# Gathers that wait for their own row tile, and context rows added by two engines in the last two batches, in a one-core transformer kernel

## Chip, cores and metric

One Trainium2 chip, one core. The metric is device time in microseconds (us) of one launch. The kernel is written instruction by instruction for five engines (TensorE, VectorE, ScalarE, GpSimd and SyncE, which issues loads); the engines meet only at semaphores. In the profile they are PE (PEld for its weight loads), DVE, ACT, POOL and SP.

## What is computed

The input `x` has 8 batches of 512 rows of 256 numbers (f32), the context 64 rows for each batch. Four steps follow each other, each of the form `x = x + tanh(g) * f(layernorm(x))`:

```python
x = x + tanh(g0) * cross_attention(ln(x), ctx)           # biased by fside
x = x + tanh(g1) * experts(ln(x))                        # a shared expert, and the best 2 of 8 by a router
# the step that this change is about, for each batch:
txt_proj = ctx @ Ws                                      # 64 x 256
feat_proj = ln(x) @ W                                    # 512 x 256
h = tanh(txt_proj[:, None] + feat_proj[None] + b)        # 64 x 512 x 256
rho = h . w                                              # 64 x 512, then masked and a softmax over the 64
txt_h = softmax(rho) @ ctx
x = x + tanh(g2) * (tanh(txt_h @ Wcw + bcw) * ln(x) + tanh(txt_h @ Wcb + bcb))
x = x + tanh(g3) * (quantized(ln(x)) @ ternary + bias)
```

## The kernel before

**Work.** All rows of `x` stay in SBUF. The kernel runs through three stages that overlap. In the first, batch by batch, attention, routing and the shared expert are done, and each row is scattered to DRAM at two places, sorted by expert. In the second, 71 "routed tiles" of 128 rows follow: each loads its rows and 1.5 MB of its expert's weights, goes through `turn_rows`, `gate`, `up`, `gate_act` and `narrow`, and its result is stored to DRAM by a DMA that POOL issues (`narrow` on POOL, L554). In the third, for each batch b the results come back: eight gathers (two for each of the four row tiles of 128 rows; L566, POOL), eight `add` steps (DVE, L953), a layer norm (`stats`, `aggr`, `power`, `newton`, `scale`, `turn`; DVE, but the power is POOL's, L534, and the transposes are PE's), and `feature` (PE L1278, copied by DVE at L960 to `featT`).

**Units.** The `tanh` of a batch is cut into 64 units (two halves ec of the 256 columns, 32 numbers m). A unit is 128x1024: two context rows against 512 rows of x. ACT does it as two instructions of 128x512 (L643, L644), each with the context row as its bias. PE then multiplies the unit by `w` (`sum`, L1291, eight matmuls). A ring of 16 buffers holds units (`wide`): unit u may be written when the sum of unit u-16 is done. After the last unit of a batch comes `mix_out` (softmax over rho, the affine, a layer norm, quantizing, the ternary product, the output).

**Units added beforehand.** For the last two batches (b of 6 and 7) `added(b, m)` is true for odd m. There DVE adds the context rows first (`preadd`, L969 and L970, two 128x512 tensor_scalar instructions, from and to SBUF, with a per-partition scalar), and ACT needs one instruction of 128x1024 (L635) in place of two.

**Order.** `Plan` writes down every step of the work at a place on one line, and each engine executes its steps in the order of these places, after `LAGS` has shifted a kind of step on one engine. Engines do not reorder: a step that waits holds all that is behind it on that engine. Places are counted in slots. The third stage begins at slot 0 of this text (`zero` in the code): batch b has slots 64b to 64b+64, and one unit has one slot. A routed tile has 8 slots, tile 22 begins at slot 0. On POOL and PE, `narrow` of tile r stands at 8r - 161.3: that of tiles 68, 69 and 70 (the last) at 382.7, 390.7 and 398.7. `tanh` of unit i of a batch is at 64b + i + 0.5 with a lag of 1.5 on ACT, `preadd` of unit i at 64b + i - 2, less 1.5 on DVE.

**The way into a batch before.** `mix_in` places the eight gathers, the adds, the norm and `feature` as equal steps: for batch 0 from slot -46 to -1, for a later one from 39.5 slots before its first slot to 3 before it. The add of gather j stands five steps behind it. The first gather of a batch waits until every tile that any row of the batch can lie in is stored: for batch 0 the first 15 tiles:

```python
tiles = 2 * ST * (b + 1) + E - 1
if j == 0:
    e.wait_ge(s_found, b + 1)
    for r in range(OUTS):
        e.wait_ge(s_stored[r], 16 * len(range(r, tiles, OUTS)))
```

Of the kernel before, what the change touches and what calls it, by code (L numbers as in the profile page):

```python
# [9 lines left out]
ALU = mybir.AluOpType  # L10
# [23 lines left out]
PLACES = {"attend": 72, "route": 36, "late": -59, "mix_first": -46, "mix_in": 24.5, "mix_in_end": -3, "feature": 3, "sum": 5,  # L34
          "mix_out": 8.5, "mix_out_end": 52.5}
# [5 lines left out]
    "scalar": {"gate_act": -2.5, "soft_rho": 1, "softmax": -2, "spread": 7.5, "squash": 2, "tanh": 1.5, ("turn", "mix"): -0.5,  # L41
               "turn_e": 1.5},
    "vector": {"add": 0.5, "add_bias": 1.5, "affine": 0.5, ("aggr", "att"): 2.5, ("aggr", "lin"): -0.5, "choice": -1.5,
               "convert": -10.5, "find": 3, "gate_act": 3, "linear": 1.5, "narrow": 2, ("newton", "att"): 2, ("newton", "lin"): 2,
               ("newton", "mix"): 0.5, ("newton", "moe"): 1, "place": -0.5, ("power", "att"): 3, "preadd": -1.5, "quantize": 1,
               ("scale", "moe"): -0.5, "side": 3.5, "softmax": 0.5, ("stats", "att"): 2.5, "step": 2, "sums": 2.5, "text": 10.5,
               ("turn", "moe"): -0.5, "turn_q": 1.5, "turn_rows": 2, "weigh": -1, "weigh_ws": -0.5},
    "tensor": {"count": -1.5, "scores": -0.5, "spread": 2.5, "sum": 1, "text": 1.5, ("turn", "mix"): -0.5, "weigh": -2},
# [3 lines left out]
class Plan:  # L52
# [16 lines left out]
    def chain(self, name, b, steps, start, end):  # L69

        self.chains[name, b] = {s for step in steps for s in step}
        self.place(steps, start, end)
# [70 lines left out]
    def added(self, b, m):  # L143

        return b >= self.B - 2 and m % 2 == 1

    def arrange(self):
# [7 lines left out]
        for b in range(B):  # L155
            at = PERIOD * b
            self.chain("attend", b, self.attend(b), at - PLACES["attend"], at - PLACES["attend"] + PERIOD - 2)
            self.chain("route", b, self.route(b), at - PLACES["route"], at - PLACES["route"] + PERIOD)
# [15 lines left out]
        for b in range(B):  # L174
            at = zero + N * b
            if b == 0:
                place([[("find", b)]], at - 60, at - 60)
                self.chain("mix_in", b, self.mix_in(b), at + PLACES["mix_first"], at - 1)
            else:
                place([[("find", b)]], at - N + 18, at - N + 18)  # L180
                self.chain("mix_in", b, self.mix_in(b), at - N + PLACES["mix_in"], at + PLACES["mix_in_end"])
# [8 lines left out]
            if b < B - 1:  # L190
                self.chain("mix_out", b, self.mix_out(b), at + N + PLACES["mix_out"], at + N + PLACES["mix_out_end"])
            else:
                self.chain("mix_out", b, self.mix_out(b), at + N + 1, at + 2 * N)
# [54 lines left out]
def build(nc, a):  # L248
# [20 lines left out]
    with ctx:  # L269
# [123 lines left out]
        s_wide_in, s_wide, s_sum = sem("wide_added"), sem("wide_tanh"), sem("rho_product")  # L393
# [113 lines left out]
        def gpsimd(e):  # L507
# [20 lines left out]
            for name, *k in plan.of["gpsimd"]:  # L528
# [13 lines left out]
                elif name == "pad":  # L542
# [3 lines left out]
                    for j in range(h * E // 2, (h + 1) * E // 2):  # L546
                        e.indirect_dma_start(
                            out=rows_dram, out_offset=bass.IndirectOffsetOnAxis(ap=pad_at[:, j:j + 1], axis=0),
                            in_=zero_tile[:, :], in_offset=None).then_inc(s_padded, 16)
                elif name == "narrow" and is_routed(k[0]):  # L550
# [4 lines left out]
                elif name == "gather":  # L555
# [3 lines left out]
                    tiles = 2 * ST * (b + 1) + E - 1  # L559
# [806 lines left out]
```

## Time and profile before

| what | us |
|---|---|
| three runs | 1123.75, 1125.29 (median), 1131.14 |
| the profiled execution, its own time | 1128.25 |
| its span, first to last instruction | 1126.5 |
| ACT busy in the span | 704.4 |
| PE / DVE / POOL busy | 1007.1 / 664.9 / 213.4 |
| mean granted TensorE clock, of full speed | 0.970 |

The busy times are sums over the whole span. The three stages have different limits, so they have to be read from windows of the trace, not from this table.

### The profile page before, as it was taken

Reading aid. Unit: us, or ns where it says so; the run is one execution under the profiler, and the core shown is the slowest. Engines: PE = TensorE matmul, PEld = TensorE weight load, DVE = VectorE, ACT = ScalarE, POOL = GpSimd, SP = SyncE. Lnnn points to the kernel's source line nnn. Section 1 sums busy time; section 2 is a strip of 40 time slices with the busy share of each in tenths; the row PEclk is TensorE's granted clock in tenths of the full one; section 3 lists DMA queues with packets and bytes.
Section 4 is the critical chain, followed back from the end, with each engine's and each line's share of the span. In section 5 each row is a group of like instructions: output and inputs, shape, how many; then the busy total and the mean of one; then the engine's idle time right before and its main releaser. Section 6 shows DMA issues by size and latency. Waiting matters only on the chain.

```text
span 1126.5 us, 23210 instructions
## 1 busy us (share of the span) xinstructions
PE 1007.1 (89%) x8772; PEld 768.6 (68%) x8772; DVE 664.9 (59%) x1902; ACT 704.4 (63%) x1154; POOL 213.4 (19%) x257
## 2 busy tenths in 40 slices
PE   6789999999889999999999999999999999948561
PEld 2467777778779998877777777777777777513120
DVE  2567778887723345434276266366366466796746
ACT  1211111111101110699999999999999999999990
POOL 1033212333320003031030030030030030120000
PEclk9969999999989999999999999999999999989995
DMA  8011110111167999766466466466466564010000
GB/s 247 24 61 61 52 40 32 43 38 38 43 239 243 336 335 340 265 228 200 139 231 215 144 223 216 156 211 215 166 202 214 176 197 145 21 33 20 1 20 19
DMA packets 114050, 164.19 MB, mean 146 GB/s; under 512 B 13235, under 2 KB 70068, under 8 KB 113940
## 3 DMA queue, kind: packets, MB, share of 16 engines
q1 hardware_dynamic: 104004, 135.57, 36.3%
q0 software_dynamic: 9936, 27.15, 6.6%
q8 instruction: 70, 1.15, 0.4%
q14 instruction: 40, 0.33, 0.1%
HBM read 138.69 MB, written 23.99 MB: 144 GB/s over the span
## 4 chain that ended last, share of the span: by engine, by line
PE 53%; ACT 27%; DVE 11%; issue 8%; DMA 0%; POOL 0%; SPq 0%; POOLq 0%; DVEq 0%
PE bank L1108 16%; PE bank L1291 9%; PE bank L1270 8%; PE bank L1113 5%; ACT tanhs L644 4%; ACT tanhs L643 4%; ACT arena L643 3%; ACT arena L644 3%; PE bank L1261 3%; ACT shared_w L644 2%; ACT shared_w L643 2%; PE bank L1150 2%; PE bank L1094 2%; PE bank L1165 2%; ACT tanhs L635 2%
## 5 line engine op out<-in xcount | busy, mean ns | idle before, releaser
L1108 PE MATMUL bank<-rowsT,expert_w 128*128 128x128 f32 x2272 | 277.1, 275 | 0.5 <-DVE rowsT L917 0.5
L1108 PEld LDWEIGHTS bank<-rowsT,expert_w 128*128 128x128 f32 x2272 | 270.0, 192 | 7.2 <-issue 3.3
L628 ACT ACTIVATE act<-bank 128x512 f32<-128x512 f32 x103 | 63.5, 616 | 217.3 <-PE bank L1108 112.6
L934 DVE COPY rows_out<-bank 128x256 f32<-128x256 f32 x71 | 30.1, 424 | 192.8 <-PE bank L1270 192.8
L1270 PE MATMUL bank<-expert_w,act 128*128 128x256 f32 x568 | 139.4, 388 | 0.8 <-issue 0.8
L554 POOL DMA_DIRECT2D expert_rows<-rows_out x71 | 40.2, 566 | 511.6 <-DVE rows_out L934 511.0
L643 ACT ACTIVATE tanhs<-arena,txtT 128x512 f32<-128x512 f32 x168 | 128.3, 764 | 4.3 <-DVE arena L960 4.3
L644 ACT ACTIVATE tanhs<-arena,txtT 128x512 f32<-128x512 f32 x168 | 128.3, 764 | 0.0
L1113 PE MATMUL bank<-normT,shared_w 128*128 128x256 f32 x512 | 125.0, 392 | 0.0
L1270 PEld LDWEIGHTS bank<-expert_w,act 128*128 128x128 f32 x568 | 102.3, 190 | 32.7 <-issue 21.7
L643 ACT ACTIVATE arena<-arena,txtT 128x512 f32<-128x512 f32 x144 | 110.0, 764 | 0.0
L644 ACT ACTIVATE arena<-arena,txtT 128x512 f32<-128x512 f32 x144 | 109.9, 764 | 0.0
L1113 PEld LDWEIGHTS bank<-normT,shared_w 128*128 128x128 f32 x512 | 97.1, 196 | 16.9 <-issue 3.3
L1291 PE MATMUL bank<-tanhs,pick_w 128*32 128x256 f32 x1536 | 97.1, 382 | 12.8 <-ACT tanhs L644 7.0
L1291 PE MATMUL bank<-arena,pick_w 128*32 128x256 f32 x1280 | 88.8, 391 | 13.3 <-ACT arena L644 6.8
L539 POOL DMA_INDIRECT rows_by_expert<-arena,slot_of x64 | 63.5, 992 | 133.7 <-DVE slot_of L844 116.6
L1291 PEld LDWEIGHTS bank<-tanhs,pick_w 128*32 128x32 f32 x1536 | 45.3, 109 | 59.4 <-ACT tanhs L644 13.1
L924 DVE SCALAR_TENSOR_TENSOR act<-act,bank 128x512 f32<-128x512 f32 x103 | 70.9, 688 | 11.6 <-DVE act L922 0.5
L1291 PEld LDWEIGHTS bank<-arena,pick_w 128*32 128x32 f32 x1280 | 38.6, 111 | 48.3 <-ACT arena L644 12.1
L922 DVE SCALAR_TENSOR_TENSOR act<-act,bank 128x512 f32<-128x512 f32 x103 | 69.7, 677 | 0.9 <-ACT act L628 0.9
L566 POOL DMA_INDIRECT picked<-expert_rows,found_at x64 | 64.3, 1005 | 28.6 <-issue 18.4
L1261 PE MATMUL bank<-shared_w,act 128*128 128x256 f32 x256 | 63.6, 392 | 6.8 <-DVE act L924 6.8
(232 smaller groups left out, 1444.0 us busy)
## 6 DMA issues: line engine op xcount, KB each, us to landing
expert_w<-in_WgT SPq DMA_DIRECT2D x71, 512.0 KB, 4.0
expert_w<-in_WuT SPq DMA_DIRECT2D x71, 512.0 KB, 5.2
expert_w<-in_WdT SPq DMA_DIRECT2D x71, 512.0 KB, 6.7
rows_in<-rows_by_expert SPq DMA_DIRECT2D x71, 128.0 KB, 5.4
expert_rows<-rows_out POOLq DMA_DIRECT2D x71, 128.0 KB, 4.3
x<-in_x SPq DMA_DIRECT2D x8, 512.0 KB, 5.5
out<-x SPq DMA_DIRECT2D x16, 256.0 KB, 4.7
score<-in_fside SPq DMA_DIRECT2D x8, 128.0 KB, 2.3
```

The costliest lines, as they stand in the source:

```text
L539: e.indirect_dma_start(out=rows_dram, out_offset=bass.IndirectOffsetOnAxis(ap=slot_of[j][:, ST * b + i:ST * b + i + 1], axis=0), in_=held[ ...
L566: e.indirect_dma_start(out=picked[u % PICKED][:, :], out_offset=None, in_=outs_dram[0:tiles * P, :], in_offset=bass.IndirectOffsetOnAxis(a ...
L628: e.activation(act[n % 2][:, :], banks[2 * (n % 2)][:, :], ACT.Tanh, scale=0.5).then_inc(s_tanh, 1)
L643: e.activation(w[:, 0:S], featT[ec], ACT.Tanh, bias=txtT[:, ec, t:t + 1])
L644: e.activation(w[:, S:2 * S], featT[ec], ACT.Tanh, bias=txtT[:, ec, t + 1:t + 2]).then_inc(s_wide, 1)
L922: link(e.scalar_tensor_tensor(out=h[:, :], in0=h[:, :], scalar=1.0, in1=bg[:, :], op0=ALU.add, op1=ALU.mult))
L924: linked(lambda: e.scalar_tensor_tensor(out=h[:, :], in0=h[:, :], scalar=0.5, in1=bu[:, :], op0=ALU.mult, op1=ALU.mult)).then_inc(s_h, 1)
L1108: got = e.matmul(bank[:, i * P:(i + 1) * P], w[:, at:at + P], t[:, c * P:(c + 1) * P], start=c == 0, stop=c == DC - 1)
L1113: got = e.matmul(bank[:, i * HALF:(i + 1) * HALF], shared_w[:, at:at + P], normT[b % 2][:, c * S + h * HALF:c * S + (h + 1) * HALF], start ...
L1261: got = e.matmul(shared_bank[:, i * D:(i + 1) * D], act[n % 2][:, c * HALF + i * P:c * HALF + (i + 1) * P], shared_w[:, at:at + D], start= ...
L1270: got = e.matmul(row_bank[:, 0:D], act[n % 2][:, c * P:(c + 1) * P], w[:, at:at + D], start=c == 0, stop=c == IC - 1)
L1291: got = e.matmul(rho_bank[32 * j:32 * j + 32, 0:H], pick_w[:, ec, 31 - m:63 - m], wide[u % WIDE][:, j * H:(j + 1) * H], start=(ec, m) == ( ...
```

## The change

The first gather of each row tile of 128 rows waits, and only for the tiles that rows up to its own row tile can lie in: for batch 0 these are 9, 11, 13 and 15 tiles for row tiles 0 to 3. Gathers, adds and the statistics (now one row tile at a time) become a chain of their own (`collect`): each add stands two steps behind its gather. For batch 0 it runs from slot -71 to -25.5, and the rest of the norm and `feature` from -25.5 to -1. For a later batch, collecting runs from 53 to 20 slots before its first slot, the rest from 20 to 3 before it. The second `feature` (ec of 1) moves from slot 3 to slot 20 of the batch, and `feature` gets a lag of -2 on PE. `find` of batch 0 moves from slot -60 to -70, with its lag of 3 on DVE.

In the last two batches every unit is added beforehand: odd m by DVE, at i - 1.5 less 1.5, and even m by POOL, at i - 3. Each engine has a semaphore of its own for this. A number of other lags change.

```diff
-PLACES = {"attend": 72, "route": 36, "late": -59, "mix_first": -46, "mix_in": 24.5, "mix_in_end": -3, "feature": 3, "sum": 5,
-          "mix_out": 8.5, "mix_out_end": 52.5}
+PLACES = {"attend": 72, "route": 36, "late": -59, "gather_first": -71, "norm_first": -25.5, "gather": 11, "norm": 44, "mix_in_end": -3,
+          "feature": 20, "sum": 5, "vector": 1.5, "gpsimd": 3, "mix_out": 8, "mix_out_end": 50.5}
...
# LAGS, the entries that change:
# scalar: squash 2 -> 0.5
# vector: convert -10.5 -> -20.5, linear 1.5 -> 5, (newton, mix) 0.5 -> 1, side 3.5 -> -3.5, (stats, mix) 0 -> 1.5,
#         step 2 -> 0.5, sums 2.5 -> 3.5
# tensor: feature 0 -> -2, text 1.5 -> 7
...
+    def collect(self, b):
+
+        steps = []
+        for i in range(self.ST + 1):
+            for j in range(2):
+                steps.append(([("gather", b, 2 * i + j)] if i < self.ST else []) + ([("add", b, 2 * i - 2 + j)] if i else []))
+            if i:
+                steps[-1].append(("stats", "mix", b, i - 1))
+        return steps
+
     def mix_in(self, b):
-        pairs = 2 * self.ST
-        steps = [[("gather", b, j)] + ([("add", b, j - 5)] if j >= 5 else []) for j in range(pairs)]
-        return steps + [[("add", b, j)] for j in range(pairs - 5, pairs)] + self.norm("mix", b) + [[("feature", b, 0)]]
+        return self.norm("mix", b)[1:] + [[("feature", b, 0)]]
...
     def added(self, b, m):
 
-        return b >= self.B - 2 and m % 2 == 1
+        if b >= self.B - 2:
+            return ("gpsimd", "vector")[m % 2]
+        return None
...
             for i, (ec, m) in enumerate(pairs):
                 if self.added(b, m):
-                    place([[("preadd", b, ec, m)]], max(at, at + i - 2), max(at, at + i - 2))
+                    early = max(at, at + i - PLACES[self.added(b, m)])
+                    place([[("preadd", b, ec, m)]], early, early)
...
+                elif name == "preadd" and plan.added(k[0], k[2]) == "gpsimd":
+                    preadd(e, "gpsimd", *k)
...
                 elif name == "gather":
-                    tiles = 2 * ST * (b + 1) + E - 1
+                    tiles = 2 * (ST * b + j // 2 + 1) + E - 1
                     if j == 0:
                         e.wait_ge(s_found, b + 1)
+                    if j % 2 == 0:
                         for r in range(OUTS):
                             e.wait_ge(s_stored[r], 16 * len(range(r, tiles, OUTS)))
...
                     if plan.added(b, m):
-                        e.wait_ge(s_wide_in, wide_in_no[u] + 1)
+                        e.wait_ge(s_wide_in[plan.added(b, m)], wide_in_no[u] + 1)
                         e.activation(w, w, ACT.Tanh).then_inc(s_wide, 1)
...
+        def preadd(e, engine, b, ec, m):
+
+            u = unit_of(b, ec, m)
+            w = wide[u % WIDE]
+            bank, use, _ = misc["feature", b, ec]
+            e.wait_ge(s_misc[bank], use)
+            if u >= WIDE:
+                e.wait_ge(s_sum, u - WIDE + 1)
+            t = b * T + 2 * m
+            e.tensor_scalar(w[:, 0:S], featT[ec], txtT[:, ec, t:t + 1], None, ALU.add)
+            e.tensor_scalar(w[:, S:2 * S], featT[ec], txtT[:, ec, t + 1:t + 2], None, ALU.add).then_inc(s_wide_in[engine], 1)
...
                     elif kind == "mix":
-                        e.wait_ge(s_added, 2 * ST * (b + 1))
+                        e.wait_ge(s_added, 2 * ST * b + 2 * part[0] + 2)
...
-                    for i in range(ST):
+                    for i in part or range(ST):
                         link(e.bn_stats(own["stats"][:, i, :], xt(b)[:, i, :]))
```

## Rows read from the trace of the kernel before

**Rows 1.** Busy us by stretch: PE, PEld, DVE, ACT, POOL; then clock, DMA share, GB/s

```profile
500.00:600.00 100.00, 98.52 (x1063) 74.71 (x1062) 50.73 (x132) 100.00 (x169) 19.34 (x23) 1.00 0.60 201
958.15:1028.00 69.85, 49.71 (x597) 25.12 (x595) 59.70 (x161) 69.85 (x100) 13.10 (x13) 0.93 0.10 30
1028.00:1099.40 71.40, 46.58 (x595) 15.98 (x591) 41.66 (x114) 71.34 (x101) 1.53 (x1) 0.98 0.03 9
```

**Rows 2.** Waits from 461 to 955 us: total us, times, longest

```profile
ACT tanhs L643 <- DVE arena L960: 4.3, 1, 4.3
```

**Rows 3.** Timeline of ACT where the first batch's units begin

```profile
start us, us, engine line op out<-in xcount [idle before <-releaser]
461.38 0.72 ACT L643 ACTIVATE tanhs<-arena,txtT 128x512 f32<-128x512 f32 x1 [4.29 <-DVE arena L960]
...
465.07 0.58 ACT L628 ACTIVATE act<-bank 128x512 f32<-128x512 f32 x1
```

**Rows 4.** Timeline of ACT: first unit of batch 6, and three of batch 7

```profile
958.15 0.85 ACT L643 ACTIVATE tanhs<-arena,txtT 128x512 f32<-128x512 f32 x1
...
1070.07 1.04 ACT L635 ACTIVATE tanhs<-tanhs 128x1024 f32<-128x1024 f32 x1
1071.02 0.71 ACT L643 ACTIVATE arena<-arena,txtT 128x512 f32<-128x512 f32 x1
...
1072.24 1.04 ACT L635 ACTIVATE arena<-arena 128x1024 f32<-128x1024 f32 x1
```

**Rows 5.** Timeline of DVE around the adds of batch 0

```profile
423.53 0.42 DVE L934 COPY rows_out<-bank 128x256 f32<-128x256 f32 x1 [3.09 <-PE bank L1270]
...
429.05 0.42 DVE L934 COPY rows_out<-bank 128x256 f32<-128x256 f32 x1 [3.09 <-PE bank L1270]
...
435.74 0.48 DVE L953 SCALAR_TENSOR_TENSOR x<-picked,share,x 128x256 f32<-128x256 f32 x1 [4.26 <-DMA picked<-expert_rows,found_at]
...
437.63 0.42 DVE L934 COPY rows_out<-bank 128x256 f32<-128x256 f32 x1
```

**Rows 6.** Timeline of PE: after these adds, and around the first feature product

```profile
438.19 0.41 PE L1223 MATMUL bank<-ident,rows_in 128*128 128x128 f32 x2 [1.87 <-issue]
...
456.95 1.95 PE L1108 MATMUL bank<-rowsT,expert_w 128*128 128x128 f32 x16
458.73 1.88 PE L1278 MATMUL bank<-mixT,feat_w 128*128 128x512 f32 x4
```

**Rows 7.** Timeline of POOL: first two gathers, and the last three stores

```profile
429.76 1.02 POOL L566 DMA_INDIRECT picked<-expert_rows,found_at  x1 [4.97 <-DMA expert_rows<-rows_out]
431.09 0.97 POOL L566 DMA_INDIRECT picked<-expert_rows,found_at  x1 [0.30 <-issue]
...
959.47 0.61 POOL L554 DMA_DIRECT2D expert_rows<-rows_out  x1 [9.87 <-DVE rows_out L934]
970.75 0.54 POOL L554 DMA_DIRECT2D expert_rows<-rows_out  x1 [10.67 <-DVE rows_out L934]
977.15 0.74 POOL L554 DMA_DIRECT2D expert_rows<-rows_out  x1 [5.86 <-DVE rows_out L934]
```

**Rows 8.** POOL's groups by form: its only elementwise work without the power

```profile
L514 POOL TENSOR_SCALAR_AFFINE_SELECT ident<-ident 128x128 f32<-128x128 f32 x1 | 0.3, 284 | 0.2 <-POOL ident L511 0.2
L511 POOL MEMSET ident<- 128x128 f32 x1 | 0.2, 205 | 0.3 <-POOLq L1356 0.3
L1356 POOL MEMSET const-float32-1.0<- 128x1 f32 x1 | 0.1, 97 | 0.0
```

**Rows 9.** Timeline: a power of POOL beside DVE's added units, and one alone

```profile
1062.37 0.48 DVE L969 TENSOR_SCALAR tanhs<-arena,txtT 128x512 f32<-128x512 f32 x1
1062.77 0.48 DVE L970 TENSOR_SCALAR tanhs<-arena,txtT 128x512 f32<-128x512 f32 x1
...
1062.55 1.53 POOL L534 TENSOR_TENSOR ln_lin_r<-ln_lin_var,halves 128x4 f32<-128x4 f32 x1 [47.28 <-DVE ln_lin_var L737]
...
1111.07 1.01 POOL L534 TENSOR_TENSOR ln_lin_r<-ln_lin_var,halves 128x4 f32<-128x4 f32 x1 [46.99 <-DVE ln_lin_var L737]
```

More of the change, by code:

```diff
@@ L40 @@
     "gpsimd": {},
-    "scalar": {"gate_act": -2.5, "soft_rho": 1, "softmax": -2, "spread": 7.5, "squash": 2, "tanh": 1.5, ("turn", "mix"): -0.5,
+    "scalar": {"gate_act": -2.5, "soft_rho": 1, "softmax": -2, "spread": 7.5, "squash": 0.5, "tanh": 1.5, ("turn", "mix"): -0.5,
                "turn_e": 1.5},
     "vector": {"add": 0.5, "add_bias": 1.5, "affine": 0.5, ("aggr", "att"): 2.5, ("aggr", "lin"): -0.5, "choice": -1.5,
[L44 to L48, printed above, removed]
+               "convert": -20.5, "find": 3, "gate_act": 3, "linear": 5, "narrow": 2, ("newton", "att"): 2, ("newton", "lin"): 2,
+               ("newton", "mix"): 1, ("newton", "moe"): 1, "place": -0.5, ("power", "att"): 3, "preadd": -1.5, "quantize": 1,
+               ("scale", "moe"): -0.5, "side": -3.5, "softmax": 0.5, ("stats", "att"): 2.5, ("stats", "mix"): 1.5, "step": 0.5,
+               "sums": 3.5, "text": 10.5, ("turn", "moe"): -0.5, "turn_q": 1.5, "turn_rows": 2, "weigh": -1, "weigh_ws": -0.5},
+    "tensor": {"count": -1.5, "feature": -2, "scores": -0.5, "spread": 2.5, "sum": 1, "text": 7, ("turn", "mix"): -0.5, "weigh": -2},
 }
@@ L67, in __init__, with chain @@
         self.count()
-    def chain(self, name, b, steps, start, end):
-        self.chains[name, b] = {s for step in steps for s in step}
-        self.place(steps, start, end)
+    def chain(self, name, b, *parts):
+        self.chains[name, b] = {s for steps, _, _ in parts for step in steps for s in step}
+        for part in parts:
+            self.place(*part)
     def check(self):
@@ L392, in build @@
         s_added = sem("x_expert_added")
-        s_wide_in, s_wide, s_sum = sem("wide_added"), sem("wide_tanh"), sem("rho_product")
+        s_wide_in, s_wide, s_sum = {e: sem(f"wide_added_{e}") for e in ("vector", "gpsimd")}, sem("wide_tanh"), sem("rho_product")
         s_rho, s_rho_sub, s_rho_e = sem("rho_read"), sem("rho_less_max"), sem("rho_exp")
@@ L716, in vector @@
                 elif name == "stats":
-                    kind, b = k
+                    kind, b, *part = k
                     own = ln_of(kind, b)
@@ L960, in vector @@
                     e.tensor_copy(featT[ec], bank[:, :]).then_inc(done, 1)
-                elif name == "preadd":
-                    b, ec, m = k
-                    u = unit_of(b, ec, m)
-                    w = wide[u % WIDE]
-                    bank, use, _ = misc["feature", b, ec]
-                    e.wait_ge(s_misc[bank], use)
-                    e.wait_ge(s_sum, u - WIDE + 1)
-                    t = b * T + 2 * m
-                    e.tensor_scalar(w[:, 0:S], featT[ec], txtT[:, ec, t:t + 1], None, ALU.add)
-                    e.tensor_scalar(w[:, S:2 * S], featT[ec], txtT[:, ec, t + 1:t + 2], None, ALU.add).then_inc(s_wide_in, 1)
+                elif name == "preadd" and plan.added(k[0], k[2]) == "vector":
+                    preadd(e, "vector", *k)
                 elif name == "rho":
```

21 lines of the change are left out of this document (12 added, 9 removed).

## The prediction

> **What bounds the kernel now.** I read the stretches first, then the waits, then the timelines. The table by stretch shows ACT busy for 100 of 100 us in the middle of the third stage, for 69.85 of 69.85 us in batch 6 and for 71.34 of 71.40 us in batch 7 [rows 1]. PE is nearly as full in the middle (98.52 of 100) but not in batches 6 and 7 (49.71 of 69.85, 46.58 of 71.40), since the last routed tile is stored at 977.15 [rows 7]. Between 461 and 955 us ACT's one wait for its tanh input is that ahead of the very first unit, 4.3 us [rows 2]. So from 461.38 us [rows 3] to about 1099.4, where the stretch of batch 7 ends, the time is ACT's work laid end to end, and PE has little to spare beneath it. What follows is the last output, some 27 us to the end of the span, which the change doesn't shorten. Two things can move the end: when the first unit starts, and what ACT spends on a unit.
>
> **What a unit costs ACT.** By start times, a unit of two instructions takes 1.22 us (1071.02 to 1072.24) and an added one 0.95 us (1070.07 to 1071.02) [rows 4]. A pair takes 2.17 us now and would take 1.90 with both added. 32 units in each of two batches change: 64 x 0.27 = 17.3 us less, 8.6 a batch. ACT does nothing else in that time, so all of it counts if the added units arrive in time. That is the question.
>
> **The start.** Today the first gather waits 4.97 us for the fifteenth tile's store [rows 7]. The first add then stands waiting on DVE (4.26 us), and the copy L934 of a routed tile stands behind it: it starts 8.58 us after the one before, where the regular distance is 5.52 [rows 5]. PE shows the same loss, with a 1.87 us idle ahead of its next transposes [rows 6]. That is 3.1 us. With a wait for 9 to 13 tiles and the first gather some 24 slots earlier, the stores are long done. A slot here is 5.52 / 8 = 0.69 us. A gather takes 6.0 us to land (429.76 to 435.74) [rows 5, 7]. The add stands two steps of 4.55 slots, 6.3 us, behind its gather in the plan, but the first gather is held by `find`, which comes to stand at slot -67, so DVE will still wait a little at the first two adds. DVE has 3.09 us free before each such copy [rows 5], which hides most of it. I count 2.5 of the 3.1 us as saved (0 to 3.1).
>
> Next, the first feature product stands behind the up product of tile 21 today (456.95, then 458.73) [rows 6]. With its new place (-4.75, where that up product has -4) it comes ahead of it, 1.8 us earlier. But three units later ACT does tile 22's gate activation (465.07 [rows 3]), whose product PE does not get to sooner by this, so I count 1.0. Start: **-3.5 us** (-5 to +1, since the moved lags of the first stage could also cost PE a little). The extra load on the DMA queues is nothing new: the same eight gathers run, only earlier. The adds and statistics are the same instructions, cut differently. In the middle batches gathers and the norm also move, but ACT has no gap there to close, so I put this at zero (-1 to +3: PE at 98.5% could be pushed behind ACT).
>
> **What POOL needs for a unit.** The trace has no tensor_scalar of POOL. The nearest rows are a memset of 128x128 (205 ns) against one of 128x1 (97 ns), 0.85 ns an element, and an affine_select, which also reads, with 284 ns, or 1.47 ns an element over the same start cost [rows 8]. For 512 elements that makes 0.53 and 0.85 us, so a unit of two costs 1.06 to 1.70 us. I take 0.65 an instruction, 1.3 a unit, nearer to the memset, since part of the affine_select's excess over it will be a fixed cost of reading. The Trainium skill's "GPSIMD Engine Reference" (section 3.1) gives 1.03 cycles an element for simple bodies bound by the port. With the memset's start cost that is an estimate of 0.54 us, and about 2 us less in the sum. POOL's rows for 128x128 neither reach this size nor have a scalar operand, so the trace can't say more.
>
> **Where POOL comes too late in batch 6.** POOL's queue is in order. (a) The store of tile 69 stands at slot 390.7, the added units from the tenth on behind it (10 - 3 = 7, slot 391). That store goes out at 970.75 and takes 0.54 [rows 7]. So unit 10 is ready at 971.3 + 1.3 = 972.6. At the new pace ACT would want it at 958.15 + 10 x 0.95 + 0.5 (one gate activation) = 968.1 [rows 4]: 4.5 us lost. It includes the first unit's own lateness, as that stands behind the store of tile 68 at 959.47. The store of tile 70 (977.15) is in time for the units behind it. (b) From slot 395 to about 420 batch 7's eight gathers come in between, 1.33 us apart (429.76 to 431.09) [rows 7]. In 24 slots POOL has 12 x 1.3 + 8 x 1.33 + 1.2 for a power = 27.4 us to do, ACT 12 x 1.90 = 22.8. Of the 4.6 missing, 1.1 are won back beforehand (three pairs at 1.90 - 1.3, less the 0.7 of a store): 3.5 lost. Batch 6: -8.6 + 4.5 + 3.5 = **-0.6 us** (with 1.06 a unit -3.7, with 1.70 +4.6). Batch 7 has only two powers beside its units: POOL 32 x 1.3 + 3 = 45 us, ACT 32 x 1.90 = 61. I leave 0.5 for late units: **-8.1 us**.
>
> **Sum.** -3.5 - 0.6 - 8.1 = -12.2 us from the profiled execution's own 1128.25 (span 1126.5 and 1.75 around it), 1116.05. That execution lies 2.96 us above the median of the runs shown, 1125.29, so the median should come to 1125.29 - 12.2 = **1113 us**. This kernel's times can be told from no change at about 1%, 11 us: the forecast is just beyond it.
>
> **Rival 1: POOL and DVE stand in each other's way, and it gets slower.** A power on four numbers takes 1.01 us alone and 1.53 us while DVE runs its adds end to end, 0.40 us apart [rows 9]. So there is something they share, and 0.52 us can be lost on one tiny instruction. The forecast has only some of this in its 1.3. If the two engines' large instructions exclude each other entirely, a pair costs 2 x 0.40 + 2 x 0.65 = 2.10 us, near the 2.17 of today. Other DVE work from SBUF comes on top: DVE is busy 59.70 us in batch 6 and 41.66 in batch 7 [rows 1], of which the 32 units are 32 x 0.80 = 25.6. If half of the rest excludes POOL too, that is 17 and 8 us. Batch 6: 67.2 + 17 + 10.6 (gathers) = 95 against 69.9, +25. Batch 7: 67.2 + 8 = 75 against 71.4, +4. With the start's -3.5: +25, **1151 us**. It decides from the point where a pair passes 2.17. Without the other DVE work: batch 6 +8, batch 7 -4, no change, **1125**. For it: rows 9. Against it: DVE's own instructions in the same row keep 0.48 us, so POOL waits there and not DVE, and exclusion need not last as long as an instruction's whole span. The Trainium skill's "SBUF — State Buffer" (section "Who interferes with whom") calls the port pair of these engines an exclusive lock, and whoever comes second blocks fully. By that rule, this rival is the outcome. The lengthened power agrees with a lock; how long one lasts, no row shows.
>
> **Rival 2: POOL is only slow.** At 1.70 a unit, batch 6 is +4.6 and batch 7 still holds 1.90 a pair but is late at its beginning, -7: with the start -6, **1119 us**. For it: the affine_select [rows 8].
>
> **Rival 3: POOL keeps up everywhere.** If its instructions overlap so that a unit takes 1.0 us or less and PE's stores come a little sooner, only some 3 us are lost in batch 6: -3.5 - 17.3 + 3 = -18, **1107 us**; with a start of -5 and no loss, 1103. Against it: the store of tile 69 is PE's to give.
>
> **How the numbers follow.** Forecast 0.45, spread 1108 to 1118; rival 1 0.22, of which 0.15 slower than 1136 and the rest near 1125; rival 2 0.18; rival 3 0.15. Faster by over 1% (below 1114): rival 3 and some six tenths of the forecast and a little of rival 2, 0.45. Slower by over 1%: 0.16. Within: 0.39. The range for 8 in 10 is 1103 to 1136, the upper end reaching into rival 1, the lower holding all of rival 3.
>
> **What would show it.** ACT's first unit near 457 us; L934 at its regular 5.5 us through the adds of batch 0. New L969 and L970 instructions on POOL, 0.55 to 0.75 us apart: above 0.95 apart, ACT is bound by POOL in both batches. Waits of ACT's L635 on POOL's units, 8 us in all, in batch 6, one right behind the last stores and one among batch 7's gathers, and almost none in batch 7. If instead L969 and L970 on DVE grow well beyond 0.48 us, rival 1 is at work. The forecast is wrong if ACT waits in batch 7, or if it starts its first unit no sooner.

## Result: 7.5% slower, because POOL sets the pace of both last batches

The changed kernel takes 1212.88 us (median of 4 runs, 1207.96 to 1213.43) against 1127.94 us for the kernel before in the same set of runs: ratio 1.0746, 95% interval 1.0694 to 1.0798. The forecast was 1113, its range ended at 1136, and the sign was wrong as well. The profiled execution takes 1213.38 us, its span is 1211.6, and the mean granted TensorE clock is 0.900 where it was 0.970.

In code lines of the changed kernel: `preadd` is L684 and L685 on both engines, the ACT instruction of an added unit L652, the pair of a unit not added L660 and L661, the store L570, the gather L583, the add L983, the copy of a routed tile L964, the copy to `featT` L990.

First the table of busy us by stretch, of the changed kernel, with columns as in [rows 1]:

```profile
500.00:600.00 100.00, 98.58 (x1086) 76.46 (x1079) 51.87 (x139) 100.00 (x168) 16.90 (x21) 1.00 0.58 197
955.00:1060.00 105.00, 46.74 (x450) 17.77 (x438) 73.23 (x138) 56.06 (x60) 103.24 (x67) 0.64 0.05 16
1060.00:1140.00 80.00, 45.97 (x398) 13.34 (x398) 48.42 (x94) 47.90 (x51) 80.00 (x49) 0.61 0.01 4
```

The middle of the third stage is what it was in [rows 1]: ACT 100 of 100 us, PE 98.58. From batch 6 on ACT, which was idle there for less than 0.1 us, works 56 of 105 and 48 of 80 us, and POOL, which had 13 and 1.5 us of work in a batch, is busy for 80 of 80. PE's granted clock has a mean of 0.64 and 0.61 in these stretches, so for most of the time it is at the lower of its two levels (1.2 and 2.4 GHz), while PE is busy for less than six tenths of the time. That is no cause of the loss: PE is waiting, as the next view shows.

The waits of the same kernel from 945 to 1190 us (total us, times, longest), those of ACT for its tanh input and one of PE's own:

```profile
PEld bank L1313 <- ACT tanhs L652: 39.6, 26, 3.5
ACT tanhs L652 <- POOL tanhs L685: 39.4, 23, 4.3
ACT arena L652 <- POOL arena L685: 35.4, 24, 2.5
...
ACT normT L652 <- POOL normT L685: 12.2, 8, 2.6
ACT shared_w L652 <- POOL shared_w L685: 11.7, 8, 2.3
```

ACT waits for POOL 63 times in 64 units, 98.7 us in all, and the sums on PE (L1313) wait for ACT. No row has ACT wait for an add of DVE. PE's longest waits are others, 41.5 us in two, for the output chain on DVE. They hold nothing up here: POOL, whose buffers PE's sums free, has 0.2 us of waits for PE in this window. The reason is in POOL's groups by form (busy us, mean ns of one):

```profile
L684 POOL TENSOR_SCALAR tanhs<-arena,txtT 128x512 f32<-128x512 f32 x24 | 41.8, 1743 | 0.3
L684 POOL TENSOR_SCALAR arena<-arena,txtT 128x512 f32<-128x512 f32 x24 | 40.9, 1706 | 0.1
```

One add costs POOL 1.71 us (219 us for all 128), not 0.65, and the instructions follow each other without a gap. The timelines of POOL and of ACT near 1088 us show the steady state:

```profile
1087.38 1.56 POOL L684 TENSOR_SCALAR arena<-arena,txtT 128x512 f32<-128x512 f32 x1
1088.91 1.56 POOL L685 TENSOR_SCALAR arena<-arena,txtT 128x512 f32<-128x512 f32 x1
```

```profile
1087.43 2.00 ACT L652 ACTIVATE arena<-arena 128x1024 f32<-128x1024 f32 x2 [1.33 <-POOL arena L685]
1090.51 2.00 ACT L652 ACTIVATE arena<-arena 128x1024 f32<-128x1024 f32 x2 [1.07 <-POOL arena L685]
```

ACT does two units in 2.00 us, then waits 1.07 until POOL has the next one: a pair takes 3.08 us at best, where the kernel before took 2.17 [rows 4].

The account of the two profiled executions closes with three numbers. ACT begins batch 6 at 954.84 (958.15 before): -3.3. From there to the end of its last unit it needs 228.9 us (to 1183.76) where it needed 141.2 (to 1099.34): +87.7. The rest of the span is 27.8 against 27.2: +0.7. Sum +85.1, the difference of the spans.

### The profile page after: what moved, and what is told of

Same layout as the page of the kernel before. It is cut to its first block, busy times and chain, and to the rows that moved or that the text cites. A ratio compares the mean times of both kernels' runs of the same rounds, so it can differ in the third digit from the quotient of the medians.

```text
span 1211.6 us, 23370 instructions
## 1 busy us (share of the span) xinstructions
PE 1031.8 (85%) x8772; PEld 770.8 (64%) x8772; DVE 716.5 (59%) x1902; ACT 693.2 (57%) x1090; POOL 427.8 (35%) x385
## 4 chain that ended last, share of the span: by engine, by line
ACT 34%; PE 33%; DVE 12%; issue 10%; POOL 9%; DMA 1%; SPq 0%; POOLq 0%; DVEq 0%
PE bank L1130 7%; ACT tanhs L661 6%; PE bank L1135 5%; ACT arena L660 5%; ACT tanhs L660 5%; ACT arena L661 5%; PE bank L1292 4%; PE bank L1313 3%; ACT shared_w L661 3%; PE bank L1283 3%; ACT shared_w L660 2%; ACT normT L660 2%; ACT normT L661 2%; PE bank L1116 2%; POOL tanhs L685 2%
## 5 line engine op out<-in xcount | busy, mean ns | idle before, releaser
L1130 PE MATMUL bank<-rowsT,expert_w 128*128 128x128 f32 x2272 | 276.7, 275 | 0.5 <-DVE rowsT L947 0.5
L1130 PEld LDWEIGHTS bank<-rowsT,expert_w 128*128 128x128 f32 x2272 | 270.4, 192 | 10.0 <-issue 6.2
L570 POOL DMA_DIRECT2D expert_rows<-rows_out x71 | 40.5, 570 | 497.0 <-DVE rows_out L964 497.0
L964 DVE COPY rows_out<-bank 128x256 f32<-128x256 f32 x71 | 30.0, 422 | 168.3 <-PE bank L1292 168.3
L1313 PE MATMUL bank<-tanhs,pick_w 128*32 128x256 f32 x1536 | 106.4, 423 | 20.6 <-ACT tanhs L652 20.6
L660 ACT ACTIVATE tanhs<-arena,txtT 128x512 f32<-128x512 f32 x144 | 111.1, 771 | 2.5 <-DVE arena L990 2.5
L661 ACT ACTIVATE tanhs<-arena,txtT 128x512 f32<-128x512 f32 x144 | 111.1, 771 | 0.0
L1313 PE MATMUL bank<-arena,pick_w 128*32 128x256 f32 x1280 | 93.4, 410 | 20.3 <-ACT arena L652 15.9
L660 ACT ACTIVATE arena<-arena,txtT 128x512 f32<-128x512 f32 x120 | 92.6, 772 | 0.0
L661 ACT ACTIVATE arena<-arena,txtT 128x512 f32<-128x512 f32 x120 | 92.6, 772 | 0.0
L1313 PEld LDWEIGHTS bank<-tanhs,pick_w 128*32 128x32 f32 x1536 | 46.8, 117 | 70.8 <-ACT tanhs L652 39.6
L1313 PEld LDWEIGHTS bank<-arena,pick_w 128*32 128x32 f32 x1280 | 35.5, 113 | 65.3 <-ACT arena L652 32.5
L583 POOL DMA_INDIRECT picked<-expert_rows,found_at x64 | 64.0, 1000 | 25.3 <-issue 17.3
L652 ACT ACTIVATE tanhs<-tanhs 128x1024 f32<-128x1024 f32 x48 | 48.5, 1053 | 39.4 <-POOL tanhs L685 39.4
```

Source lines behind the costliest of these rows:

```text
L583: e.indirect_dma_start(out=picked[u % PICKED][:, :], out_offset=None, in_=outs_dram[0:tiles * P, :], in_offset=bass.IndirectOffsetOnAxis(a ...
L652: e.activation(w, w, ACT.Tanh).then_inc(s_wide, 1)
L660: e.activation(w[:, 0:S], featT[ec], ACT.Tanh, bias=txtT[:, ec, t:t + 1])
L661: e.activation(w[:, S:2 * S], featT[ec], ACT.Tanh, bias=txtT[:, ec, t + 1:t + 2]).then_inc(s_wide, 1)
L1130: got = e.matmul(bank[:, i * P:(i + 1) * P], w[:, at:at + P], t[:, c * P:(c + 1) * P], start=c == 0, stop=c == DC - 1)
L1313: got = e.matmul(rho_bank[32 * j:32 * j + 32, 0:H], pick_w[:, ec, 31 - m:63 - m], wide[u % WIDE][:, j * H:(j + 1) * H], start=(ec, m) == ( ...
```

## Experiments

The ratios are to the kernel before in the same set of runs, whose median was 1128.05 us in the first set (e1 to e4), 1136.72 in the second (e5, e6, e7, e9), 1127.71 in the third (e8, e10) and 1135.33 in the fourth (e11, e5b).

### e1: all of the change but POOL's units

```diff
     def added(self, b, m):
-        if b >= self.B - 2:
-            return ("gpsimd", "vector")[m % 2]
+        if b >= self.B - 2 and m % 2:
+            return "vector"
```

> All of the change but POOL's added units: in the last two batches only odd m is added beforehand, by DVE, as before; gathers, places and lags are the new ones. If the whole loss comes from POOL's units and the first unit's earlier start (457.15 against 461.38 us) is kept to the end: 4 us faster than before, about 1124 us, and 85 to 90 us faster than the changed kernel. If the new places cost something in the middle batches or for the late units: no faster than before, 1128 us or more.

Measured: 1123.38 us, ratio 0.9959 [0.9938, 0.9981], which is -4.6 us, between -7.0 and -2.1. Batch 6 in its table by stretch:

```profile
952.27:1024.00 71.73, 50.76 (x586) 21.65 (x578) 58.37 (x159) 71.73 (x103) 12.48 (x12) 0.88 0.09 27
```

ACT is full in batch 6 again. So the new gathers, places and lags are worth a small gain, and the whole loss comes with POOL's units.

### e2: the kernel before, with POOL's units alone

The kernel before, with even m of the last two batches added by POOL as in the change (`"vector": 2, "gpsimd": 3` as places, two semaphores), and nothing else.

> The kernel before with POOL adding the even units of the last two batches, nothing else. If POOL's units are the whole loss: 1128 + 89 = about 1217 us. If they only hurt in the company of the new places and lags: well below 1200 us.

Measured: 1215.45 us, ratio 1.0776 [1.0742, 1.0811]. With e1 this makes the two parts of the change add up: 1.0776 x 0.9959 = 1.0732, and the whole change has 1.0746.

### e3: POOL's units, but none on DVE

```diff
-        if b >= self.B - 2:
-            return ("gpsimd", "vector")[m % 2]
+        if b >= self.B - 2 and m % 2 == 0:
+            return "gpsimd"
```

> The changed kernel with POOL's units but none of DVE's: odd m is left to ACT with its bias. Theory: POOL's instruction is slow by itself, 1.54 us start to start; its spans fall from a mean of 1.70 to nearly 1.56 us and 128 of them take 199 us in place of 218: about 1193 us, still POOL-bound. Rival: the two engines exclude each other and this sets POOL's pace; then without DVE's adds POOL's instructions fall well below 1 us, ACT is the bound again and the time is about 1125 us (1128 - 4, no saving on the odd units but the same on the even).

Measured: 1197.12 us, ratio 1.0609 [1.0583, 1.0635]. Taking all of DVE's adds away returns (1.0746 - 1.0609) x 1128 = 15.5 us. One stretch of it, and the durations of L684 on POOL (min/median/max ns, first and last start):

```profile
1060.00:1100.00 40.00, 27.84 (x250) 7.20 (x242) 8.48 (x19) 30.32 (x43) 40.00 (x27) 0.67 0.00 1
```

```profile
L684 POOL TENSOR_SCALAR tanhs<-arena,txtT x24: 1552/1553/1784, 947.0 to 1144.3; 128x512 f32<-128x512 f32 x24
```

With DVE busy for 8.48 of 40 us, POOL still works for 40.00 of 40, at 1.55 us an instruction. So POOL's own price is the cause, and what DVE does to it is the smaller part.

### e4: what POOL's instructions cost by themselves

The kernel before, with 19 POOL instructions ahead of everything, in which DVE does nothing (they are extra work, so its time of 1146.2 us has no meaning of its own). The comments stand here only; L530 to L534 are the other five kinds in their order.

```diff
+            kinds = [lambda to: e.tensor_scalar(to, fro, one, None, ALU.add)] * 3       # L528, scalar per partition
+            kinds += [lambda to: e.tensor_scalar(to, fro, 1.0, None, ALU.add)] * 3      # L529, constant
+            kinds += [lambda to: e.tensor_scalar(to[:, 0:256], fro[:, 0:256], one, None, ALU.add)] * 2
+            kinds += [lambda to: e.tensor_scalar(to[:, 0:128], fro[:, 0:128], one, None, ALU.add)] * 2
+            kinds += [lambda to: e.tensor_copy(to, fro)] * 3
+            kinds += [lambda to: e.memset(to, 0.0)] * 3
+            kinds += [lambda to: e.tensor_tensor(to, fro, other, ALU.add)] * 3
```

> The kernel before with 19 instructions of POOL ahead of everything, where DVE waits for POOL's constants and does nothing: 128x512 tensor_scalar with a per-partition scalar (3) and with a constant (3), the former with 256 and 128 columns (2 each), copy (3), memset (3) and tensor_tensor (3) of 128x512. Theory: the per-partition tensor_scalar takes 1.55 us alone too, some 3 ns an element (128 columns near 0.5 us), and the memset 0.53 us, as worked out from 128x128. Rival: alone it takes 0.6 to 0.8 us, and what the changed kernel shows is contention. The constant's form tells whether the scalar operand is what costs: then it takes about 0.6 us, else also 1.5. The whole kernel some 20 us longer than before.

POOL's groups by form from 4 to 23 us (busy us, mean ns):

```profile
L528 POOL TENSOR_SCALAR arena<-tanhs 128x512 f32<-128x512 f32 x3 | 4.7, 1566 | 0.1
L529 POOL TENSOR_SCALAR arena<-tanhs 128x512 f32<-128x512 f32 x3 | 4.4, 1488 | 0.0
L534 POOL TENSOR_TENSOR tanhs<-tanhs 128x512 f32<-128x512 f32 x3 | 3.7, 1264 | 0.0
L530 POOL TENSOR_SCALAR arena<-tanhs 128x256 f32<-128x256 f32 x2 | 1.8, 928 | 0.0
L533 POOL MEMSET tanhs<- 128x512 f32 x3 | 1.5, 532 | 0.0
...
L531 POOL TENSOR_SCALAR arena<-tanhs 128x128 f32<-128x128 f32 x2 | 1.2, 608 | 0.0
L532 POOL COPY arena<-tanhs 128x512 f32<-128x512 f32 x2 | 1.2, 616 | 0.0
```

The memset of 512 comes out at 532 ns, just where the prediction's 0.85 ns an element had put it, and a copy at 616. The tensor_scalar takes 608, 928 and 1566 ns for 128, 256 and 512 elements: (1566 - 608) / 384 = 2.5 ns an element and some 0.29 us at the start. The two instructions that were in the trace of before are cheap ones and this one isn't: at 128x128 the affine_select had 284 ns [rows 8] and the tensor_scalar has 608. It is even dearer than the add of two tensors, 1264 ns.

### e5: a smaller dose, a quarter of batch 7's units on POOL

```diff
+        if b >= self.B - 2 and m % 2:
+            return "vector"
+        if b == self.B - 1 and m % 4 == 0:
+            return "gpsimd"
```

> As e1_no_pool_units (1123.4 us), but in the last batch POOL adds every fourth unit (m divisible by 4, 16 units), DVE the odd ones as before. POOL then has 2 x 1.55 to 2 x 1.75 = 3.1 to 3.5 us of work in every four units, which take ACT 2 x 0.95 + 0.95 + 1.22 = 4.07 us. Theory (rate): where POOL is not asked for more than it can do, an added unit saves ACT its 0.27 us whoever adds it: 16 x 0.27 = 4.3 us, about 1119 us, no waits of ACT on POOL beyond the first unit. Rival (contention): POOL's instructions hold up DVE's adds and its other work so that ACT waits for DVE's units: 1123 us or more.

Measured: 1128.16 us, ratio 0.9923 [0.9897, 0.9948]. Within the fourth set, as e5b, with this on record,

> The same kernel as e5_pool_quarter_b7, on the chip of the run above, so that the two differ by batch 6 alone. Both theories: 0.990 to 0.995 of the kernel before.

it took 1123.59 us, ratio 0.9911 [0.9882, 0.9940]. Against e1's ratio these are 4.1 and 5.4 us less, but both intervals overlap e1's a little, and the chips differ. The traces are clearer: from ACT's first unit of batch 7 to the end of its last one e1 takes 70.4 us (1022.93 to 1093.34), e5 66.6 and e5b 66.0, which is 3.9 and 4.4 less; 16 units at 0.27 us are 4.3. In the middle of batch 7 ACT is full, and POOL is at 49.88 of 60 us:

```profile
1030.00:1090.00 60.00, 37.65 (x478) 14.39 (x474) 51.32 (x110) 59.53 (x77) 49.88 (x30) 0.89 0.03 10
```

So the arithmetic of what an added unit saves ACT holds, as long as POOL gets one unit in four (3.1 to 3.9 us of work in two pairs of ACT's, 1.90 + 2.17 = 4.07 us) and not one in two.

### e6: the same dose on DVE

e5 with `m % 4 == 2` and `"vector"` in its last two lines.

> As e1_no_pool_units, but in the last batch DVE also adds the units with m of 2, 6, 10, ... (16 more units of 0.80 us: its 41.7 us of work in some 67 become 54.5). If ACT's 0.27 us a unit is all that counts: 4.3 us less than e1, about 1119 us. If DVE's order makes the units late (they stand behind mix_out's chain): no gain over e1's 1123.

Measured: 1128.90 us, ratio 0.9941 [0.9918, 0.9964]; DVE is busy 51.00 of the same 60 us and ACT 60.00. ACT's batch 7 takes 66.0 us (1036.05 to 1102.01), 4.5 less than in e1, so at this dose it doesn't matter which engine adds. The whole time shows less of it: 2.0 us below e1's ratio, which is within the two intervals.

### e7: all units of batch 7 added, POOL's as one instruction with two inputs

```diff
+        if b == self.B - 1:
+            return "gpsimd" if m % 4 == 0 else "vector"
...
+            if engine == "gpsimd":
+                both = [P, 2, S]
+                e.tensor_tensor(w.rearrange("p (t s) -> p t s", t=2), featT[ec].unsqueeze(1).to_broadcast(both),
+                                txtT[:, ec, t:t + 2].unsqueeze(2).to_broadcast(both), ALU.add).then_inc(s_wide_in[engine], 1)
+                return
```

> As e1_no_pool_units, but in the last batch all units are added: every fourth by POOL, and by one tensor_tensor of 128x1024 (feature and context row both repeated by their access patterns) in place of two tensor_scalar instructions, the other three by DVE. By e4's price of 1.23 us for 512 elements POOL's instruction should take about 2.2 us, against 3.80 us that ACT needs for four units; DVE has 48 x 0.80 + 16 = 54.5 us for 61. If rates are all that counts: 32 x 0.27 = 8.6 us less than e1, about 1115 us. If the two engines hold each other up at this load (DVE's adds at 0.82 to 0.90 us beside POOL's, as in the changed kernel): 1119 to 1125 us.

Measured: 1135.46 us, ratio 0.9997 [0.9975, 1.0019]. The form with two inputs is much cheaper for POOL: 1.89 us for both context rows at best, where two tensor_scalar take 3.12. But the gain of e1 is gone. The timeline shows why:

```profile
1069.24 1.89 POOL L688 TENSOR_TENSOR arena<-arena,txtT 128x1024 f32<-128x1024 f32 x1
...
1069.33 1.82 DVE L780 TENSOR_TENSOR ln_lin_t<-ln_lin_t,ln_lin_var 128x4 f32<-128x4 f32 x1
```

A DVE instruction on four numbers, which takes 0.16 us where POOL is idle, starts just behind POOL's, takes 1.82 us, and ends with it. From 1030 to 1090 us DVE is busy for 59.09 us and ACT for 46.35. Here the exclusion of rival 1 is to be seen in full, and it is DVE that loses. This form differs from the tensor_scalar in three ways (a second tensor as input, inputs that are repeated, twice the length), and no run separates them.

### e8 and e10: the same cheap form in the change itself, with and without DVE's units

e8 is the changed kernel with the `tensor_tensor` of e7 for each of POOL's units; e10 is e8 with `added` as in e3.

> The changed kernel, with POOL's unit as one tensor_tensor of 128x1024 (1.89 us at least, 2.16 in the mix, as in the run with all units of batch 7 added) in place of two tensor_scalar (3.42 us). Theory (only the price of POOL's instructions was wrong in the prediction): 64 units at some 2.1 us are 134 us, with the eight gathers and the stores of batch 6 about 148, against the 141 us that batches 6 and 7 take in the kernel before; with the earlier start of 4.6 us the end comes at about +3 us: ratio 0.995 to 1.01. Rival (the engines' exclusion, which two instructions with two inputs show in full): DVE's two adds of a pair (0.8 us) and its other work (about 30 us in batch 6, 16 in batch 7) don't run beside POOL: a pair is 2.8 us or more, the two batches take about 190 us, +45 us: ratio 1.03 to 1.05, and DVE's adds then show instructions of more than 1.5 us.

> The kernel of the run above, but odd units are left to ACT with two instructions, so DVE adds none. A pair costs ACT 0.95 + 1.22 = 2.17 us and POOL 2.0 to 2.2. Theory of the price: POOL hardly later than ACT, batch 7 as before, batch 6 some 8 us longer for the gathers, start -4.6: ratio 0.995 to 1.01. Rival (exclusion): DVE's other work (30 us in batch 6, 16 in batch 7) is added to POOL's 64 x 2.0: about +25 us, ratio 1.015 to 1.03. If it is near 1.00 while the run above is at 1.03 or more, it is DVE's adds, and not its other work, that POOL can't run beside.

Measured: e8 1191.42 us, ratio 1.0569 [1.0529, 1.0610]; e10 1152.15 us, ratio 1.0230 [1.0182, 1.0279]. The theory that only the price counted falls in both; in e8 even the rival is exceeded. POOL's instruction costs 1.96 to 1.98 us in e8, so its 64 units are 125 us and not 219, and yet only 20 us are won of the 85. In e8's groups from 1060 to 1140 us and its timeline, DVE pays:

```profile
L690 DVE TENSOR_SCALAR tanhs<-arena,txtT 128x512 f32<-128x512 f32 x10 | 16.2, 1620 | 0.0
```

```profile
1086.28 0.40 DVE L1020 TENSOR_REDUCE sm_rmax<-rhos 128x4 f32<-128x256 f32 x1
...
1088.07 4.10 POOL L686 TENSOR_TENSOR arena<-arena,txtT 128x1024 f32<-128x1024 f32 x2
1088.31 2.11 DVE L689 TENSOR_SCALAR tanhs<-arena,txtT 128x512 f32<-128x512 f32 x1
```

The 0.48 us add of DVE takes 2.11, one whole POOL instruction. The reduction at 1086.28 isn't held: it takes 0.40 us, and POOL is busy with three such adds from 1082.15 to 1088.11. ACT now waits for DVE and hardly for POOL (ACT's waits in e8 from 945 to 1165 us):

```profile
ACT sm_ws L669 <- DVE sm_bs L1034: 26.4, 2, 16.9
ACT arena L652 <- DVE arena L690: 18.2, 6, 6.8
...
ACT arena L652 <- POOL arena L686: 4.3, 2, 3.3
```

e10, where DVE adds nothing, still loses 26 us, the 2.3% that its rival gave. The chain that ended last shows how, at the end of batch 5's output (start, us, what):

```profile
1002.42 8.29 DVE out_work L1074 x2
...
1016.11 1.01 PE bank L1333 x8
1017.12 4.76 PE bank L1318 x56
```

Two DVE instructions that take 0.41 us each in e1 take 8.29 together, and four of POOL's adds run from 1002.79 to 1010.22. PE's queue has the ternary product (L1333) that waits for them ahead of its sums (L1318), so no buffer of the ring comes free, and POOL (8.09 us idle) and ACT (6.72) stand still as well. Between e8 and e10 lie 3.4%: DVE's adds.

### e9: only the waits of the gathers

The kernel before with `tiles = 2 * (ST * b + j // 2 + 1) + E - 1` and the wait at each even j, in the old places.

> The kernel before with nothing changed but the gathers' waits (at the first gather of a row tile, for its own tiles only). It tells apart what gave e1's 4.6 us. If it is the waits: the first gather no longer waits 4.97 us for the 15th store, DVE's adds block L934 less and ACT's first unit comes 2 to 3 us sooner: about 1125 us. If it is the places (adds further behind their gathers, the first feature product ahead of the up product): the first unit stays near 461 us, 1128 us.

Measured: 1135.28 us, ratio 0.9995 [0.9978, 1.0012], no change. POOL's timeline around the fifteenth tile's store:

```profile
433.86 0.54 POOL L554 DMA_DIRECT2D expert_rows<-rows_out  x1 [4.96 <-DVE rows_out L935]
434.73 1.02 POOL L567 DMA_INDIRECT picked<-expert_rows,found_at  x1 [0.33 <-issue]
```

The 4.97 us of [rows 7] are gone. But the first unit comes 35.9 us after this store, where it came 37.1 and 36.4 after it in the two profiles with the old waits: 0.4 to 1.2 us. DVE's rows show where the rest went:

```profile
442.46 0.48 DVE L954 SCALAR_TENSOR_TENSOR x<-picked,share,x 128x256 f32<-128x256 f32 x1 [0.84 <-DMA picked<-expert_rows,found_at]
444.54 0.42 DVE L935 COPY rows_out<-bank 128x256 f32<-128x256 f32 x1 [1.59 <-PE bank L1271]
...
449.05 0.42 DVE L918 COPY rowsT<-bank 128x256 f32<-128x256 f32 x1 [2.08 <-remote]
...
451.62 0.43 DVE L935 COPY rows_out<-bank 128x256 f32<-128x256 f32 x1 [1.36 <-PE bank L1271]
```

The adds hardly block DVE any more: 0.84 us of waiting for a gather in place of 4.26, and the copy L935 at 444.54 is 5.88 us behind the one before it, not 8.58. But the next copy is 7.08 us behind that, with 2.08 us in which DVE waits for something that the trace does not name. So the waits alone do away with the loss at the first adds and are still worth next to nothing here, for a cause that stays open. The places without the waits were not tried.

### e11: a quarter of the units on POOL in both batches

e5 with `b >= self.B - 2` for POOL's line. It tests point (a) of the prediction, the store of tile 69 in POOL's queue, which the change itself never gets to.

> The kernel that adds a quarter of batch 7's units on POOL (ratio 0.9923), with the same quarter of batch 6 as well. POOL has 3.1 to 3.4 us for such a unit and gets one every 4.07 us of ACT, so it keeps up but for what else is in its queue. Theory (the prediction's point (a), never reached so far): the store of routed tile 69, which PE gives at about 970 us, stands ahead of unit 12 of batch 6; ACT wants that unit at about 952.3 + 12 x 1.02 + 0.5 = 965 us and has it at 970.8 + 3.2 = 974: 9 us lost in one wait, 4.3 gained by the 16 units, and some 3 lost among batch 7's gathers: ratio 0.998 to 1.003. Rival (the store doesn't hold it, since PE gives its last tiles sooner or ACT is held elsewhere): another -4.3 us, ratio 0.987 to 0.990.

Measured: 1139.20 us, ratio 1.0034 [1.0017, 1.0051]: 1.2% above e5b, so the second quarter costs more than the first one brings. The ratio is the one of the theory, but the mechanism isn't, as POOL's timeline shows:

```profile
964.99 1.72 POOL L687 TENSOR_SCALAR arena<-arena,txtT 128x512 f32<-128x512 f32 x1
966.66 0.59 POOL L572 DMA_DIRECT2D expert_rows<-rows_out  x1
967.28 1.86 POOL L686 TENSOR_SCALAR normT<-arena,txtT 128x512 f32<-128x512 f32 x1
```

POOL comes to the store without waiting, and ACT has no idle time up to 990 us. It loses its time further on, where batch 7's gathers stand between the units and DVE has the output of batch 5 to finish (ACT's waits from 945 to 1150 us):

```profile
ACT tanhs L654 <- POOL tanhs L687: 8.9, 6, 3.8
ACT shared_w L654 <- DVE shared_w L687: 5.8, 4, 2.0
```

With two small ones ahead of its units that is 16.2 us of waits; less the 4.3 gained, 12 lost, and the two batches take 150.1 us (960.52 to 1110.58) against 136.7 in e5b. 11.7 of the 13.4 us between them lie in batch 6. That the gathers and batch 5's output cause these waits is read from their place in time; no run takes either away.

## Why the prediction was wrong, by its own steps

**The step that failed is "I take 0.65 an instruction, 1.3 a unit".** It is 1.55 us where DVE is idle (e3, e4) and 1.71 in the change: 3.1 to 3.4 us a unit, twice the upper bound of 1.70 as well. Nothing in [rows 8] was misread: the memset's slope is confirmed to the nanosecond. The error was to take two instructions that happened to be in the trace, one that reads nothing and one with another operation, for bounds of a third. The text said itself that they neither reach the size nor have a scalar operand, and made a range of 0.53 to 0.85 from them all the same, where the only kind of row near to the operation, a POOL instruction with arithmetic, was the power with 1.01 us on four elements. The sentence on the Trainium skill's "GPSIMD Engine Reference" (section 3.1, 1.03 cycles an element for simple bodies) leant the same way, and e4 speaks against it for this operation: 2.5 ns an element. With the memset (532 ns) e4 agrees, and with the copy (616) nearly.

**Where POOL comes too late.** The terms of batch 6 (-8.6 + 4.5 + 3.5) and of batch 7 (-8.1) were made for an engine that is faster than ACT's pair. Above 1.90 us a unit every unit is late, and the sum of POOL's queue is the time: 128 x 1.71 = 219 us, eight gathers at 1.06 with 1.4 us between them, and the stores and powers, less small overlaps, make the 231.4 us from its first unit at 950.32 to the end of its last one at 1181.73. Instead of -8.7 the two batches have +87.7. Units late because of a store or a gather are details in this. The term for the store of tile 69 (4.5 us) was wrong also by itself. It took the store's time from the kernel before, 12.6 us behind ACT's first unit of batch 6 (970.75 against 958.15). With the new places and lags it goes out 4.0 us behind it in e1 (956.25 against 952.27) and in e5b (965.90 against 961.90), long before ACT wants the tenth unit, so even a fast POOL would have lost nothing there. In the sums for 1.06 and 1.70 us a unit the prediction also left the 1.1 us won back beforehand as they were, though they depend on the price: by its own terms batch 6 comes to -4.4 and +5.8, not -3.7 and +4.6. At 0.54 us an instruction the sum is some 3 us lower, not 2. Without the 4.5 us the forecast would have been 1109 us: none of this comes near what the price did.

**The saving of an added unit was right.** The forecast had 0.27 us a unit, 4.3 for 16. In ACT's time for batch 7 the 16 units more give 3.9 us in e5, 4.4 in e5b and, added by DVE, 4.5 in e6.

**The start.** Predicted -3.5. From the first routed tile's store to the fifteenth and on to ACT's first unit, the profile of before has 77.25 + 37.13 us, the changed one 79.62 + 32.58: -2.2. These rows are of POOL and ACT in the changed kernel:

```profile
344.95 0.60 POOL L570 DMA_DIRECT2D expert_rows<-rows_out  x1 [24.36 <-DVE rows_out L964]
...
424.57 0.58 POOL L570 DMA_DIRECT2D expert_rows<-rows_out  x1 [4.78 <-DVE rows_out L964]
```

```profile
457.15 0.72 ACT L660 ACTIVATE tanhs<-arena,txtT 128x512 f32<-128x512 f32 x1 [2.46 <-DVE arena L990]
```

The second part, 32.58, is the same to 0.01 us in all ten profiles with the new places. The part that I had at 2.5 (the adds no longer block) brought 0.7 net: DVE still waits at the first adds, now ahead of the fifteenth store,

```profile
415.30 0.49 DVE L983 SCALAR_TENSOR_TENSOR x<-picked,share,x 128x256 f32<-128x256 f32 x1 [2.42 <-DMA picked<-expert_rows,found_at]
415.96 0.42 DVE L964 COPY rows_out<-bank 128x256 f32<-128x256 f32 x1 [0.18 <-PE bank L1292]
419.16 0.48 DVE L983 SCALAR_TENSOR_TENSOR x<-picked,share,x 128x256 f32<-128x256 f32 x1 [2.77 <-DMA picked<-expert_rows,found_at]
...
423.85 0.42 DVE L964 COPY rows_out<-bank 128x256 f32<-128x256 f32 x1 [1.76 <-PE bank L1292]
```

and these two copies are 7.89 us apart instead of 5.52. The prediction had said that they would wait "a little" and that DVE's 3.09 us hide it; the second wait isn't hidden. What is left of the gain, 1.5 us, would be the feature product's, for which I had 1.0. The first batch then gives 0.9 us back: it takes ACT 83.1 us in e1 and in the change, 82.2 before, with a wait of 0.8 us for PE (L1130) that was not there. In all e1 measures -4.6, more than these -1.3. The rest would have to lie in the first stage, where lags moved too: the first store comes sooner with the new places (345.0, 341.8 and 342.0 us in three profiles, 347.0 and 343.6 without; on the chip of the second set 351.2, 353.6 and 347.5, and 356.6 in e9). But profiles of one order differ by 3.4 and by 6.2 us there, so that part stays open.

**Rival 1, rightly there and wrongly priced.** In the change, the two engines disturb each other by little. DVE's adds beside POOL's tensor_scalar take 0.90, 0.48 and 0.82 us in turn instead of 0.48, POOL's grow from 1.56 to 1.98 (six of 128 take 2.0 to 2.7), and without DVE's adds 15.5 of the 85 us go (e3). The timelines of POOL and of DVE at one place:

```profile
1069.47 1.98 POOL L684 TENSOR_SCALAR shared_w<-arena,txtT 128x512 f32<-128x512 f32 x1
```

```profile
1069.68 0.90 DVE L684 TENSOR_SCALAR tanhs<-arena,txtT 128x512 f32<-128x512 f32 x1
1070.51 0.48 DVE L685 TENSOR_SCALAR tanhs<-arena,txtT 128x512 f32<-128x512 f32 x1
1070.91 0.82 DVE L684 TENSOR_SCALAR tanhs<-arena,txtT 128x512 f32<-128x512 f32 x1
```

Three DVE adds start in the 1.98 us of one POOL instruction and two of them end in it, so it doesn't exclude them for its whole length. The tensor_tensor does (e7, e8: 2.11 us). The Trainium skill's "SBUF — State Buffer" (section "SBUF: two separate sides") says that of a POOL instruction and a DVE one that uses both ports or has two inputs in SBUF, whichever is first has the port pair for the whole instruction. e7 and e8 agree with it for POOL's two-input add (2.11 us); the rows above don't for its tensor_scalar (0.90 us).

**Rival 2** had the right mechanism, a POOL that is only slow, and 1.70 us a unit in place of 3.42. **Rival 3** is out. The section on what would show it did name the reading that came: "above 0.95 apart, ACT is bound by POOL in both batches". They are 1.54 apart and more. What it lacked was a price and a chance for that case: at 1.2 us, say, 64 x 2.4 and some 12 us of gathers and stores make 166 us against 141, which with the start is +21 us, and every further tenth of a microsecond adds 13. At the 1.71 us measured that sum gives +86, where the spans differ by 85.1.

## What to carry to other kernels

The price of an operation on an engine is measured for that operation: a memset or a select says nothing about an add with a scalar on the same engine, and where no row shows it, the range has to include the value from which the engine becomes the bound, with the time that this gives. Before half of a loop's work goes to a slow engine, compare its time for one item with the time that the bounding engine has for the items it serves: here one in four fits in batch 7 and brings 3.9 to 4.4 us (e5, e5b), the same in batch 6, where gathers and stores share the queue, costs 1.2% (e11), and one in two in both costs 7.8% (e2). And the cheapest form for one engine need not be the cheapest for the kernel: POOL's two-input add takes some 40% less than its two tensor_scalar, and DVE loses most of what that wins.

## What the hardware showed beyond that

- POOL's tensor_scalar (1566 ns for 128x512 f32 with a scalar per partition, 1488 with a constant) is slower than its tensor_tensor add of the same size (1264), and with both inputs broadcast, 128x1024 takes 1.89 us, under 1 us for 512.
- A DVE tensor_scalar or tensor_tensor caught beside POOL's two-input add takes POOL's time whatever its own size: 1.82 us for 128x4, 2.11 us for 128x512, and 8.29 us for the two in e10's chain, so it can lose its turn more than once: a 128x4 tensor_tensor (L780) at 997.14 us in e10 takes 4.39 us through two of POOL's adds. Not every DVE instruction is held: the reductions of e8 (L1020, L1026) take 0.40 to 0.42 us all through. POOL itself stays between 1.88 and 2.08 us in e8: at this meeting DVE is the one that waits.
- It goes the other way with a short POOL instruction: the power on four numbers, 1.01 us alone [rows 9], takes 2.32 and 2.33 us in e6 and e7, where DVE runs added units end to end.
